# Marks of the feed-forward part: inner columns on partitions, turned in 32x32 blocks on VectorE

## The chip, the core and the metric

The kernel runs on one core of one Trainium2 chip. Its engines are TensorE (PE in the profile, its weight loads PEld), VectorE (DVE), ScalarE (ACT), GpSimd (POOL) and SyncE (SP, which here only issues transfers). They run side by side and wait for each other on semaphores. The metric is device time in microseconds; the time before is 880.39 us, the median of 3 runs (879.23 to 880.98).

## What is computed

Four sequences of 512 tokens with 512 features go through attention and then through a feed-forward layer that is sparse by a choice within blocks. The second half is what the change touches:

```python
x = layernorm(x + attention(x))                     # 4 x 512 x 512
inter = x @ c1.T @ c2.T                             # rank 16: 512 -> 16 -> 1792
idx = argmax(inter in 56 blocks of 32, axis=-1)     # one inner column for each block
h = relu(sum_m w1[idx] * x)                         # only the chosen columns
x = layernorm(x + h @ w2t[idx])
```

The kernel does not gather. It multiplies with all of w1, and sets to zero what is not the largest of its block (of equal ones it keeps the first).

## The kernel before, in words

`_attend` does the attention and `_feed_forward` the rest. The feed-forward part takes the batches b = 0 to 3 in turn, and each in 14 rounds m of 128 inner columns; a batch has 512 tokens. Every 32-bit product is made of three matmuls of high and low parts. Each engine has its own program, written out by hand in the order in which it runs; nothing is scheduled by a tool.

TensorE's round m of batch b is: `inner_up(b, m)`, 12 matmuls of 512 columns into `ps_h` (before and after it splits into two halves of six); between the halves the first of the round's preparation steps; `first_marks(b, m)`, one matmul of the marks with a triangular matrix into `ps_z`, whose entries are 1 only at the first mark of a block; `inner_down` of the round before, 12 matmuls into the four output banks `ps_pair`, with the round's second preparation step between its halves; and last `turn_mask` for the next round, four 128x128 transposes of the marks into `ps_t`.

ScalarE applies relu to `ps_h` (L933), copies the turned marks from `ps_t` to `mask_t` (L926, function `turn`), and makes the high part `g_h` of the picked values (L940). VectorE multiplies the relu's output by (ps_z == 1), which is `pick` (L1013). GpSimd makes the low part `g_l` (L883, function `low_g`); in batch 0 it also makes the low parts of w2 (L875). `inner_down` waits for `g_l`.

The preparation steps of a batch are listed in `slot_steps`. Four (s = 0 to 3) transpose the next batch's normalized tokens and split them into high and low parts; one (U) multiplies them with c1 into `u`, 80 rows; 16 (`marks(c, t)`) make the marks: for a tile of 128 tokens and a piece of 448 of the 1792 inner columns, one matmul with tokens on the partitions (L1128), a maximum over each block of 32 (L998, 14 results) and a comparison with it (L1003), which writes a 16-bit mask. All read one PSUM bank, `ps_prep`, and TensorE waits before each for VectorE's work on the one before. VectorE does a round's first step ahead of its pick.

Within a batch b of 1 to 3 VectorE has more in rounds 0 to 2: `add(b-1)` (four additions, L1028), `statistics(b-1)` (L1033, L1039, L1041), and `norm` (L1047), each for the output of the batch before.

The way in to the rounds is a stretch in which TensorE projects the attention's output of batches 1 to 3 (`project_out`, L1141) and VectorE adds the residual (`add_residual`, L1020, L1022), normalizes (`norm`, L1047) and does batch 0's first preparation steps (`front`). SyncE stores each normalized batch and loads the next residual; batch 1's tokens for step s = 0 are loaded (L799) after all four stores have landed.

Of the kernel before, what the change touches and what calls it, by code (L numbers as in the profile page):

```python
# [27 lines left out]
P = 128  # L28
# [677 lines left out]
def _feed_forward(nc, x, x1, out, w2, w2_late, sums, rden, keep, late):  # L706
# [8 lines left out]
    marks = lambda c, t: TT + 1 + c * TT + t  # L715
    att_parts2, y0, pairs = late
    att_h, att_l = zip((xt_h[1], xt_l[1]), (xt_h[0], xt_l[0]), att_parts2, (xt_h[1], xt_l[1]))
    with ExitStack() as ctx:
# [14 lines left out]
        top = [sb(f"top{j}", [P, CH // BLK]) for j in range(2)]  # L733
        mask = sb("mask", [P, TT, INTER], BF16)
# [9 lines left out]
        ps_h, ps_z, ps_prep = ps("ps_h", [P, S]), ps("ps_z", [P, S]), ps("ps_prep", [P, S])  # L744
        ps_t = ps("ps_t", [P, S], BF16)
# [3 lines left out]
        mask_turned, mask_t_ready = sem("mask_turned"), sem("mask_t_ready")  # L749
# [15 lines left out]
        def slot_steps(b, m):  # L765

            own = {0: ((1, 0), (1, 1)), 1: ((1, 2), (1, 3)), 2: ((2, 0),), 3: ((2, 1),), 4: ((2, 2),),
                   5: ((2, 3),), 6: ((3, 0), (3, 1)), 7: ((3, 2), (3, 3))}
            ahead = {2: (0,), 3: (1,), 4: (2,), 5: (3,), 8: (U,), 9: (marks(0, 0),), 10: (marks(0, 1),),
                     11: (marks(0, 2),), 12: (marks(0, 3),)}  # L770
            out = [(b, marks(c, t)) for c, t in own.get(m, ())]
            if b < NB - 1:
                out += [(b + 1, s) for s in ahead.get(m, ())]
            return out

        FRONT = [*range(TT), U, *(marks(0, t) for t in range(TT))]
# [10 lines left out]
        def front_bank(s):  # L787

            return (ps_prep, ps_z)[FRONT.index(s) % 2]

# [129 lines left out]
        def _(act):  # L920
            def turn(b, m):
                i = b * MT + m
                act.wait_ge(mask_turned, i + 1)
                if i >= 2:
                    act.wait_ge(z_done, i - 1)
                nc.scalar.activation(mask_t[m % 2][:], ps_t[:], ACT.Copy).then_inc(mask_t_ready, 1)  # L926

# [36 lines left out]
            turn(0, 0)  # L964
            high_w2(0)
            for b in range(NB):
                for m in range(MT):
                    if b == 0 and m + 1 < MT:
                        high_w2(m + 1)
                    relu(b, m)  # L970
                    if b * MT + m + 1 < NB * MT:
                        turn(*divmod(b * MT + m + 1, MT))
                    high_g(b, m)

        @block.vector
        def _(dve):
            def step(b, s, bank):
                n = number(b, s)
                dve.wait_ge(prep_mm, n + 1)
                if s < TT:  # L980
# [7 lines left out]
                    dve.wait_ge(prep_half, n + 1)  # L988
                    nc.vector.tensor_tensor(dst[1], src, dst[0].bitcast(F32), ALU.subtract).then_inc(prep_done, 1)  # L989
                elif s == U:  # L990
                    nc.vector.tensor_copy(u[:], bank[0:80]).then_inc(prep_half, 1)
                    dve.wait_ge(prep_half, n + 1)
                    nc.vector.tensor_tensor(u[32:32 + RANK], bank[32:32 + RANK],
                                            u[32:32 + RANK].bitcast(F32), ALU.subtract).then_inc(prep_done, 1)
                else:
                    c, t = divmod(s - TT - 1, TT)
                    src = bank[:, 0:CH].rearrange("p (n k) -> p n k", k=BLK)
                    nc.vector.tensor_reduce(top[t % 2][:], src, AX.X, ALU.max).then_inc(prep_half, 1)  # L998
                    dve.wait_ge(prep_half, n + 1)
                    if b and t == 0:  # L1000

                        dve.wait_ge(mask_turned, MT * (b - 1) + min(MT, -(-(c + 1) * CH // P)))
                    nc.vector.tensor_tensor(  # L1003
                        mask[:, t, c * CH:(c + 1) * CH].rearrange("p (n k) -> p n k", k=BLK), src,
                        top[t % 2][:].rearrange("p (n o) -> p n o", o=1).broadcast_to([P, CH // BLK, BLK]),
                        ALU.is_equal).then_inc(prep_done, 1)
# [43 lines left out]
            def front(s):  # L1050
                step(0, s, front_bank(s))
# [28 lines left out]
            for b in range(NB):  # L1080
                for m in range(MT):
                    steps = slot_steps(b, m)
                    if steps:
                        step(*steps[0], ps_prep)
                    pick(b, m)
                    if len(steps) > 1:
                        step(*steps[1], ps_prep)
# [18 lines left out]
        def _(pe):  # L1106
            def step(b, s, bank, banks=1):
                n = number(b, s)
                if n >= banks:
                    pe.wait_ge(prep_done, n - banks + 1)  # L1110
# [14 lines left out]
                else:  # L1125
                    c, t = divmod(s - TT - 1, TT)
                    pe.wait_ge(prep_done, number(b, U) + 1)
                    last = nc.tensor.matmul(bank[:, 0:CH], u[:, t * P:(t + 1) * P], c2_s[:, c * CH:(c + 1) * CH],  # L1128
                                            start=True, stop=True)
                last.then_inc(prep_mm, 1)  # L1130

            def front(s):
                step(0, s, front_bank(s), 2)
# [10 lines left out]

            def turn_mask(b, m):
                i = b * MT + m

                pe.wait_ge(prep_done, number(b, marks(-(-(m + 1) * P // CH) - 1, TT - 1)) + 1)
                if i:
# [145 lines left out]
```

## Time and profile before

| | |
|---|---|
| median of 3 runs | 880.39 us |
| the profiled execution, whole | 878.44 us |
| its span, from the first to the last instruction | 876.7 us |
| TensorE busy in the span | 840.4 us (96%) |
| VectorE busy | 564.4 us (64%) |
| ScalarE busy | 416.9 us (48%) |
| GpSimd busy | 279.4 us (32%) |
| a residual's load (1024 KB), median from issue to landing | 5.5 us |

The profile shows one execution. Busy time is time in which an engine had an instruction under way. Matmuls overlap, so a matmul's duration (0.39 us) is longer than the step from one start to the next (0.23 us): what a matmul costs TensorE is read from starts. An engine's idle time costs nothing unless it holds up the engine that is needed next.

### The profile page before, as it was taken

To read this page: it belongs to the slowest core of one execution; us is meant where nothing else is said; L and a number is where in the kernel's file an instruction comes from. 1 tells how busy PE (TensorE), PEld (TensorE's weight loads), DVE (VectorE), ACT (ScalarE), POOL (GpSimd) and SP (SyncE) were. 2 spreads that over 40 slices of the span, in tenths; PEclk is the share of its full clock that TensorE was granted. 3 is DMA by queue.
4 is the path that set the end of the run, shared out by engine and by line. 5 is a ranking of instruction groups with operands and counts; after the bars stand their busy time and mean duration, and the time that the engine had idled before them with its cause. 6 is when DMAs were issued, how large, how long until landed. Compare 5 with 4: busy or idle time off the path is not lost. (4 is left out here: it accounts for less than half of the span.)

```text
span 876.7 us, 11899 instructions
## 1 busy us (share of the span) xinstructions
PE 840.4 (96%) x4316; PEld 501.7 (57%) x4344; DVE 564.4 (64%) x772; ACT 416.9 (48%) x777; POOL 279.4 (32%) x324
## 2 busy tenths in 40 slices
PE   6999999999999999999989899999999999999995
PEld 5866333333333333333347677777777777777773
DVE  5588899899999999997037965328432663345304
ACT  4321677787888788878721133332222222222231
POOL 2213235633564354114304134332112211212121
PEclk9999899999999999999999899999999999999998
DMA  7793342334553453333226433110400030002001
GB/s 215 258 285 112 101 103 81 99 110 114 152 147 111 113 145 118 85 87 100 97 80 202 156 120 97 37 49 13 133 1 1 0 121 1 1 1 96 1 1 48
DMA packets 48225, 83.07 MB, mean 95 GB/s; under 512 B 9544, under 2 KB 13640, under 8 KB 48040
## 3 DMA queue, kind: packets, MB, share of 16 engines
q1 hardware_dynamic: 40448, 64.45, 23.9%
q0 software_dynamic: 7440, 16.76, 6.3%
q10 hardware_dynamic: 280, 1.11, 0.4%
q8 instruction: 35, 0.57, 0.3%
q14 instruction: 22, 0.18, 0.1%
HBM read 54.18 MB, written 28.05 MB: 94 GB/s over the span
## 5 line engine op out<-in xcount | busy, mean ns | idle before, releaser
L517 DVE TENSOR_REDUCE neg_max<-ps_pair 128x2 f32<-128x1024 f32 x256 | 303.4, 1217 | 29.9 <-PE ps_pair L632 29.7
L483 ACT ACTIVATE probs<-ps_st 128x512 f32<-128x512 f32 x512 | 267.1, 603 | 69.9 <-PE ps_st L645 69.8
L645 PE MATMUL ps_st<-q,k 50*128 50x512 f32 x512 | 158.1, 476 | 0.5 <-ACT probs L483 0.2
L883 POOL TENSOR_TENSOR g_l<-picked,g_h 128x512 fp32r<-128x512 f32 x56 | 73.1, 1306 | 268.0 <-ACT g_h L940 268.0
L645 PEld LDWEIGHTS ps_st<-q,k 50*128 50x128 f32 x512 | 69.5, 186 | 144.8 <-ACT probs L483 141.1
L659 PE MATMUL ps_pv<-probs,v 128*32 128x512 f32 x1024 | 138.3, 612 | 0.0
L926 ACT ACTIVATE mask_t<-ps_t 128x512 bf16<-128x512 bf16 x56 | 33.4, 597 | 169.0 <-PE ps_t L1152 169.0
L632 PE MATMUL ps_pair<-k,q 48*128 48x512 f32 x512 | 106.0, 448 | 7.6 <-DVE neg_max L517 7.5
L998 DVE TENSOR_REDUCE top<-ps_prep 128x14 f32<-128x448 f32 x62 | 38.6, 623 | 98.8 <-PE ps_prep L1128 98.7
L1164 PE MATMUL ps_h<-xt_h,w_h 128*128 128x512 f32 x224 | 92.4, 413 | 0.0
L1013 DVE SCALAR_TENSOR_TENSOR picked<-ps_z,picked 128x512 f32<-128x512 f32 x56 | 38.7, 691 | 77.9 <-ACT picked L933 77.8
L1164 PE MATMUL ps_h<-xt_h,w_l 128*128 128x512 f32 x224 | 87.8, 392 | 0.0
L1164 PE MATMUL ps_h<-xt_l,w_h 128*128 128x512 f32 x224 | 87.6, 391 | 0.0
L933 ACT ACTIVATE picked<-ps_h 128x512 f32<-128x512 f32 x56 | 33.6, 600 | 110.5 <-PE ps_h L1164 110.5
L632 PEld LDWEIGHTS ps_pair<-k,q 48*128 48x128 f32 x512 | 54.2, 188 | 48.4 <-DVE neg_max L517 30.8
L1189 PE MATMUL ps_pair<-w_h,g_h 128*128 128x512 f32 x160 | 71.4, 446 | 0.0
L1189 PE MATMUL ps_pair<-w_h,g_l 128*128 128x512 f32 x160 | 63.2, 395 | 0.0
L1189 PE MATMUL ps_pair<-w_l,g_h 128*128 128x512 f32 x160 | 62.5, 390 | 0.0
L311 POOL DMA_DIRECT2D maxima<-max_rows x32 | 24.7, 772 | 108.8 <-PE ps_st L645 79.1
L321 POOL DMA_DIRECT2D q<-maxima x64 | 32.4, 514 | 79.5 <-DMA maxima<-max_rows 79.3
L1164 PEld LDWEIGHTS ps_h<-xt_h,w_l 128*128 128x128 f32 x224 | 42.0, 188 | 9.3
L1164 PEld LDWEIGHTS ps_h<-xt_h,w_h 128*128 128x128 f32 x224 | 42.3, 189 | 7.1
(146 smaller groups left out, 1144.2 us busy)
## 6 DMA issues: line engine op xcount, KB each, us to landing
operands<-parts POOLq DMA_DIRECT2D x20, 512.0 KB, 4.0
q<-operands SPq DMA_DIRECT2D x64, 128.0 KB, 2.6
sums<-stage SPq DMA_DIRECT2D x32, 256.0 KB, 2.3
x_raw<-xT SPq DMA_DIRECT2D x16, 256.0 KB, 5.0
k<-operands SPq DMA_DIRECT2D x64, 64.0 KB, 2.4
q<-operands SPq DMA_DIRECT2D x64, 64.0 KB, 2.5
att<-sums SPq DMA_DIRECT2D x16, 256.0 KB
yf<-x SPq DMA_DIRECT2D x4, 1024.0 KB, 5.5
```

What stands on the lines that cost most here:

```text
L483: nc.scalar.activation(probs[kt % 2][:, r], ps_st[i % 3][:], ACT.Exp, scale=float(HD) ** -0.5).then_inc(exp_done, 1)
L517: nc.vector.tensor_reduce(neg_max[:, at:at + 2], ps_max[pair % 2][:], AX.X, ALU.max, negate=True).then_inc(max_red, 1)
L632: nc.tensor.matmul(ps_max[tile // 2 % 2][:, a], q[n % QR][64 * a:64 * a + STACK, j, t * P:(t + 1) * P], k_[n % QR][64 * a:64 * a + STACK, ...
L645: nc.tensor.matmul(ps_st[i % 3][:], k_[n % QR][64 * a:64 * a + ROWS, kt * P:(kt + 1) * P], q[n % QR][64 * a:64 * a + ROWS, j, :], start=Tr ...
L659: last = nc.tensor.matmul(ps_pv[32 * r:32 * r + VW], v[b][:, kt, g], probs[kt % 2][:, r], start=(kt == 0), stop=(kt == TT - 1))
L883: nc.gpsimd.tensor_tensor(g_l[m % 2][:], picked[m % 2][:], g_h[m % 2][:].bitcast(F32), ALU.subtract).then_inc(g_ready, 1)
L926: nc.scalar.activation(mask_t[m % 2][:], ps_t[:], ACT.Copy).then_inc(mask_t_ready, 1)
L933: nc.scalar.activation(picked[m % 2][:], ps_h[:], ACT.Relu).then_inc(relu_ready, 1)
L998: nc.vector.tensor_reduce(top[t % 2][:], src, AX.X, ALU.max).then_inc(prep_half, 1)
L1013: nc.vector.scalar_tensor_tensor(picked[m % 2][:], ps_z[:], 1.0, picked[m % 2][:], ALU.is_equal, ALU.mult).then_inc(picked_ready, 1)
L1164: last = nc.tensor.matmul(ps_h[:], w[:, k, m * P:(m + 1) * P], xx[b % 2][:, k], start=(k == 0 and n == 0), stop=(k == KT - 1 and n == 2))
L1189: last = nc.tensor.matmul(ps_out[t][:], g[m % 2][:, t * P:(t + 1) * P], w2_tile(*w, m), start=(m == 0 and n == 0), stop=(m == MT - 1 and n ...
```

## The change

The marks are computed with inner columns on the partitions and tokens along the free dimension. A marks step now belongs to a round: `marks(m)` is one matmul of the 128 inner columns of round m with all 512 tokens (weights `c2_s`, moving data `u`), so 14 of 512 columns take the place of 16 of 448. VectorE then turns the bank in 32x32 blocks from PSUM into `turned`, which brings the 32 columns of an inner block to lie along the free dimension; it takes the maximum of each group of 32 (16 results), compares, which writes `marked` in 16 bits, and turns the blocks back into `mask_t`. TensorE's `turn_mask` (four transposes a round) and ScalarE's `turn` (one copy a round) are gone, and with them `ps_t` and the 14 KB `mask`.

Further: `u` has two buffers, by batch; the preparation steps use two banks in turn and TensorE waits for the step before the last; each round r does the marks of round r+1; VectorE does its pick first, then the marks, then the second step. On the way in one marks step stands in place of four, and VectorE's first `add_residual` of batch 2 stands ahead of batch 1's `norm`.

```diff
         def slot_steps(b, m):
...
-            own = {0: ((1, 0), (1, 1)), 1: ((1, 2), (1, 3)), 2: ((2, 0),), 3: ((2, 1),), 4: ((2, 2),),
-                   5: ((2, 3),), 6: ((3, 0), (3, 1)), 7: ((3, 2), (3, 3))}
...
+            ahead = {2: 0, 3: 1, 4: 2, 5: 3, 8: U}
+            following = (b, marks(m + 1)) if m + 1 < MT else (b + 1, marks(0))
...
+        def prep_bank(b, s):
+
+            return ps_prep[number(b, s) % 2]
...
-            def turn(b, m):
-                i = b * MT + m
-                act.wait_ge(mask_turned, i + 1)
-                if i >= 2:
-                    act.wait_ge(z_done, i - 1)
-                nc.scalar.activation(mask_t[m % 2][:], ps_t[:], ACT.Copy).then_inc(mask_t_ready, 1)
...
-                    nc.vector.tensor_reduce(top[t % 2][:], src, AX.X, ALU.max).then_inc(prep_half, 1)
...
+                    i = b * MT + s - TT - 1
+                    if i:
+                        dve.wait_ge(marks_ready, i)
+                    nc.vector.transpose(turned[:].rearrange("p n k -> p (n k)"), bank[:]).then_inc(prep_done, 1)
+                    dve.wait_ge(prep_done, n + 1)
+                    nc.vector.tensor_reduce(top[:], turned[:], AX.X, ALU.max).then_inc(topped, 1)
+                    dve.wait_ge(topped, i + 1)
+                    if i:
+                        dve.wait_ge(mask_t_ready, i)
                     nc.vector.tensor_tensor(
...
+                        marked[:], turned[:],
+                        top[:].rearrange("p (n o) -> p n o", o=1).broadcast_to([P, S // BLK, BLK]),
+                        ALU.is_equal).then_inc(marks_ready, 1)
+                    dve.wait_ge(marks_ready, i + 1)
+                    if i >= 2:
+                        dve.wait_ge(z_done, i - 1)
+                    nc.vector.transpose(mask_t[i % 2][:], marked[:].rearrange("p n k -> p (n k)")).then_inc(mask_t_ready, 1)
...
-            front(marks(0, 0))
-            front(marks(0, 1))
+            front(marks(0))
+            add_residual(2, 0)
             norm(1)
-            add_residual(2, 0)
-            front(marks(0, 2))
-            front(marks(0, 3))
...
                     steps = slot_steps(b, m)
+                    pick(b, m)
                     if steps:
-                        step(*steps[0], ps_prep)
-                    pick(b, m)
+                        step(*steps[0])
...
-                    last = nc.tensor.matmul(bank[:, 0:CH], u[:, t * P:(t + 1) * P], c2_s[:, c * CH:(c + 1) * CH],
-                                            start=True, stop=True)
+                    last = nc.tensor.matmul(bank[:], c2_s[:, m * P:(m + 1) * P], us[b % 2][:], start=True, stop=True)
...
-                    if b * MT + m + 1 < NB * MT:
-                        turn_mask(*divmod(b * MT + m + 1, MT))
```

On VectorE, from batch 1's pick of round 1 to its pick of round 2, before (marks steps L998 and L1003, statistics L1033 to L1041):

```order
L1013 SCALAR_TENSOR_TENSOR picked<-ps_z,picked 128x512 [waits relu_ready,z_done]
L998 TENSOR_REDUCE top<-ps_prep 128x14 [waits prep_mm]
L1003 TENSOR_TENSOR mask<-ps_prep,top 128x448 [waits prep_half]
L1033 BN_STATS statsf<-yf 128x6 [waits yf_ready] x4
L1039 BN_AGGR mvf<-statsf 128x2 [waits statf_done] x4
L1041 TENSOR_SCALAR varf<-mvf 128x4 [waits aggrf_done]
L998 TENSOR_REDUCE top<-ps_prep 128x14 [waits prep_mm]
L1003 TENSOR_TENSOR mask<-ps_prep,top 128x448 [waits mask_turned,prep_half]
L1013 SCALAR_TENSOR_TENSOR picked<-ps_z,picked 128x512 [waits relu_ready,z_done]
```

The same engine after the change, from one pick to the next in a round of batch 0 with a token step (marks L991 to L1004, token step L978 and L980):

```order
L1011 SCALAR_TENSOR_TENSOR picked<-ps_z,picked 128x512 [waits relu_ready,z_done]
L991 STREAM_TRANSPOSE turned<-ps_prep 128x512 [waits marks_ready,prep_mm]
L993 TENSOR_REDUCE top<-turned 128x16 [waits prep_done]
L997 TENSOR_TENSOR marked<-turned,top 128x512 [waits mask_t_ready,topped]
L1004 STREAM_TRANSPOSE mask_t<-marked 128x512 [waits z_done,marks_ready]
L978 CAST xt_h<-ps_prep 128x4x128 [waits prep_mm]
L980 TENSOR_TENSOR xt_l<-ps_prep,xt_h 128x4x128 [waits prep_half]
L1011 SCALAR_TENSOR_TENSOR picked<-ps_z,picked 128x512 [waits relu_ready,z_done]
```

A marks step has grown from two instructions to four, each waiting for the one before it, and stands behind the pick.

On TensorE, the end of one round and the start of the next, before:

```order
L1189 MATMUL ps_pair<-w_h,g_l 128x512
L1152 MATMUL ps_t<-ident,mask 128x128 [waits mask_t_ready,prep_done]
L1152 MATMUL ps_t<-ident,mask 128x128 x3
L1164 MATMUL ps_h<-xt_h,w_h 128x512 [waits relu_ready]
L1164 MATMUL ps_h<-xt_l,w_h 128x512
```

and after:

```order
L1173 MATMUL ps_pair<-w_h,g_l 128x512
L1148 MATMUL ps_h<-xt_h,w_h 128x512 [waits relu_ready]
L1148 MATMUL ps_h<-xt_l,w_h 128x512
L1148 MATMUL ps_h<-xt_h,w_l 128x512
L1148 MATMUL ps_h<-xt_h,w_h 128x512
```

The four transposes between the rounds are gone; the rest of the round keeps its order.

## Rows read from the trace of the kernel before

**Rows 1.** Busy time in a stretch of rounds: length, engines, clock, DMA, GB/s

```profile
620.00:700.00 80.00, 80.00 (x381) 61.45 (x387) 35.19 (x60) 20.92 (x37) 16.32 (x14) 1.00 0.08 25
```

**Rows 2.** Waits, 515 to 877 us, TensorE's: us in total, times, longest

```profile
PE ps_pair L1189 <- POOL g_l L883: 0.5, 1, 0.5
```

**Rows 3.** Timeline of TensorE at a round's end: start us, us, what

```profile
844.55 0.39 PE L1189 MATMUL ps_pair<-w_h,g_l 128*128 128x512 f32 x1
844.78 0.40 PE L1152 MATMUL ps_t<-ident,mask 128*128 128x128 bf16 x4
844.99 0.48 PE L1164 MATMUL ps_h<-xt_h,w_h 128*128 128x512 f32 x1
845.31 0.39 PE L1164 MATMUL ps_h<-xt_l,w_h 128*128 128x512 f32 x1
```

**Rows 4.** Timeline of TensorE at a marks matmul

```profile
691.42 0.37 PE L1128 MATMUL ps_prep<-c_s,u 80*128 80x448 f32 x1
691.63 0.40 PE L1164 MATMUL ps_h<-xt_h,w_h 128*128 128x512 f32 x1
```

**Rows 5.** TensorE's groups by form, 515 to 877 us: busy us, mean ns

```profile
L1152 PE MATMUL ps_t<-ident,mask 128*128 128x128 bf16 x212 | 21.1, 222 | 0.0
L1128 PE MATMUL ps_prep<-c_s,u 80*128 80x448 f32 x55 | 20.2, 368 | 0.0
```

**Rows 6.** VectorE's groups by form, whole span

```profile
L1013 DVE SCALAR_TENSOR_TENSOR picked<-ps_z,picked 128x512 f32<-128x512 f32 x56 | 38.7, 691 | 77.9 <-ACT picked L933 77.8
L539 DVE STREAM_TRANSPOSE max_rows<-max_parts 128x32 f32<-128x32 f32 x32 | 6.4, 201 | 0.1
```

**Rows 7.** Timelines of VectorE and GpSimd in the attention, 259 to 264 us

```profile
260.95 0.91 DVE L532 TENSOR_TENSOR max_parts<-neg_max,max_parts 128x16 fp32r<-128x16 f32 x1
262.92 0.19 DVE L539 STREAM_TRANSPOSE max_rows<-max_parts 128x32 f32<-128x32 f32 x1
...
260.56 1.27 POOL L384 TENSOR_TENSOR att<-att,inv 128x512 f32<-128x512 f32 x1
...
262.59 1.28 POOL L390 TENSOR_TENSOR xt_l<-att,xt_h 128x512 fp32r<-128x512 f32 x1
```

**Rows 8.** Timeline of the last round: relu, pick, low part

```profile
860.10 0.60 ACT L933 ACTIVATE picked<-ps_h 128x512 f32<-128x512 f32 x1 [1.69 <-PE ps_h L1164]
860.80 0.69 DVE L1013 SCALAR_TENSOR_TENSOR picked<-ps_z,picked 128x512 f32<-128x512 f32 x1 [5.35 <-ACT picked L933]
862.24 1.28 POOL L883 TENSOR_TENSOR g_l<-picked,g_h 128x512 fp32r<-128x512 f32 x1 [2.46 <-ACT g_h L940]
```

**Rows 9.** Timeline of VectorE in a batch's first rounds

```profile
603.74 2.46 DVE L1033 BATCH_NORM_STATS2 statsf<-yf 128x6 f32<-128x512 f32 x4
...
606.60 0.61 DVE L998 TENSOR_REDUCE top<-ps_prep 128x14 f32<-128x448 f32 x1
607.25 0.62 DVE L1003 TENSOR_TENSOR mask<-ps_prep,top 128x448 bf16<-128x448 f32 x1
...
610.58 1.91 DVE L1047 TENSOR_SCALAR yf<-yf,mvf,rstdf 128x512 f32<-128x512 f32 x4
...
690.01 2.48 DVE L1028 TENSOR_TENSOR yf<-ps_pair,yf 128x512 f32<-128x512 f32 x4 [0.18 <-PE ps_pair L1189]
```

**Rows 10.** Timelines of the way in: VectorE, SyncE's issues, TensorE

```profile
479.69 3.90 DVE L1047 TENSOR_SCALAR yf<-yf,mvf,rstdf 128x512 f32<-128x512 f32 x4
...
495.68 0.68 DVE L1020 TENSOR_TENSOR yf<-ps_pair,yf 128x512 f32<-128x512 f32 x1
...
504.48 3.85 DVE L1047 TENSOR_SCALAR yf<-yf,mvf,rstdf 128x512 f32<-128x512 f32 x4
...
487.80 0.38 SPq L820 DMA_DIRECT2D yf<-x  x1
...
513.08 0.33 SPq L799 DMA_DIRECT2D xf_sb<-after_attention  x1
...
516.12 0.60 PE L1118 MATMUL ps_prep<-ident,xf_sb 128*128 128x128 f32 x4
```

More of the change, by code:

```diff
@@ L732, in _feed_forward @@
         x_sb = [sb(f"xf_sb{j}", [P, D]) for j in range(2)]
[L733 to L734 removed]
+        u_next = sb("u_next", [80, S], F32R)
+        turned = sb("turned", [P, S // BLK, BLK])
+        top = sb("top", [P, S // BLK])
+        marked = sb("marked", [P, S // BLK, BLK], BF16)
         mask_t = [sb(f"mask_t{j}", [P, S], BF16) for j in range(2)]
@@ L765, in slot_steps @@
         def slot_steps(b, m):
-            own = {0: ((1, 0), (1, 1)), 1: ((1, 2), (1, 3)), 2: ((2, 0),), 3: ((2, 1),), 4: ((2, 2),),
-                   5: ((2, 3),), 6: ((3, 0), (3, 1)), 7: ((3, 2), (3, 3))}
[L769 to L773, printed above, removed]
+            ahead = {2: 0, 3: 1, 4: 2, 5: 3, 8: U}
+            following = (b, marks(m + 1)) if m + 1 < MT else (b + 1, marks(0))
+            out = [following] if following[0] < NB else []
+            if b + 1 < NB and m in ahead:
+                out.append((b + 1, ahead[m]))
             return out
-        FRONT = [*range(TT), U, *(marks(0, t) for t in range(TT))]
+        FRONT = [*range(TT), U, marks(0)]
         ORDER = [(0, s) for s in FRONT]
@@ L1050, in front @@
             def front(s):
-                step(0, s, front_bank(s))
+                step(0, s)
             add_residual(0, 0)
@@ L1106, in _, with step @@
         def _(pe):
[L1107 to L1110, printed above, removed]
+            def step(b, s):
+                n, bank = number(b, s), prep_bank(b, s)
+                if n >= 2:
+                    pe.wait_ge(prep_done, n - 1)
                 if s < TT:
@@ L1143, in project_out @@
                 last.then_inc(wo_done, 1)
[L1145 to L1149, printed above, removed]
-                    pe.wait_ge(mask_t_ready, i)
-                for t in range(TT):
-                    last = nc.tensor.transpose(ps_t[:, t * P:(t + 1) * P], mask[:, t, m * P:(m + 1) * P], ident16[:])
-                last.then_inc(mask_turned, 1)
             def inner_up(b, m, ks):
@@ L1205, in _ @@
             project_out(2, 2)
-            front(marks(0, 0))
-            front(marks(0, 1))
+            front(marks(0))
             project_out(2, 3)
-            front(marks(0, 2))
-            front(marks(0, 3))
-            project_out(3, 0)
-            project_out(3, 1)
-            turn_mask(0, 0)
-            project_out(3, 2)
-            project_out(3, 3)
+            for t in range(TT):
+                project_out(3, t)
             inner_up(0, 0, (0, 1, 2, 3))
@@ L1223, in _ @@
                     if steps:
-                        step(*steps[0], ps_prep)
+                        step(*steps[0])
                     if b * MT + m:
```

45 lines of the change are left out of this document (17 added, 28 removed).

## The prediction

> **What bounds the kernel now.** I read the busy time by stretches first. In the rounds TensorE is busy all of the time (80.00 of 80.00 us between 620 and 700) at a granted clock of 1.00, and VectorE less than half (35.19) [rows 1]. The list of waits for 515 to 877 us then has one wait of a matmul, 0.5 us in the last round [rows 2]; the other engines wait for TensorE. So in some 360 us the sum of what TensorE issues is the time, and what is taken off its queue is gained whole, as long as the others keep up. The question of this change is whether VectorE does. The way in, 480 to 515 us, is different: there VectorE is the late one, and it ends in a transfer [rows 10].
>
> **What goes on TensorE.** A round's end shows the cost of `turn_mask`. From the last matmul of `inner_down` at 844.55 to the transposes at 844.78 is an ordinary step, 0.23. The transposes hold the queue to 844.99, and the matmul behind them takes 0.32 to the next instead of 0.23 (845.31) [rows 3]. So four transposes cost 845.31 - 844.78 - 0.23 = 0.30 us. I count from one fixed point, the first token step of batch 1 (516.12, in round 2 of batch 0 [rows 10]), since from there on the order is regular. Behind it stand 53 groups of four (212 transposes [rows 5]): 53 x 0.30 = **-15.9**. A marks matmul of 448 columns takes 691.63 - 691.42 = 0.21 [rows 4], and there are 55 [rows 5]: 11.5. In their place come 52 of 512 columns at the ordinary 0.23, 12.0: **+0.5**. The token steps, U, `first_marks` and all others stay as they are.
>
> **What it costs VectorE.** Nothing in the trace is a 32x32 turn of 512 columns. Its nearest row is the turn of 32 columns, 201 ns [rows 6]. Two readings bound it. If the instruction pays a fixed part and then one element after another, as the others do (the pick takes 691 ns for 512 [rows 6], the maximum 610 for 448 [rows 9]: about 0.16 us and 1.04 ns an element), 32 elements should take 0.19, and they do; 512 would take 0.70. If each block of 32 paid the whole 201 ns, 16 blocks would take 3.2 us. Below, two elements at a time, like the norm (1.91 for four of 512, 0.48 each [rows 9]), would be 0.5. I take 0.70 since it explains the row. Maximum and comparison of 512 elements are 0.70 each by the same line. Between two that depend on each other lie 0.04 us (606.60 + 0.61 to 607.25 [rows 9]).
>
> The Trainium skill ("VectorE: DVE Perf Modes", section "The three transpose paths") gives 311 ns for VectorE's turn of 128x128 in bf16. An estimate that takes four of them for 512 columns is 1.24 us; one that takes 0.16 us as fixed is 0.76. With 1.24 twice a round the sum below would come out some 7 us longer.
>
> **A collision that the change makes.** The comparison used to read PSUM; now it reads two tiles in SBUF. The trace shows what happens to such an instruction beside GpSimd: L532, which takes 0.17 us alone, started at 260.95 while GpSimd's L384 ran from 260.56 to 261.83, and lasted 0.91, to 261.86, so it was held to GpSimd's end. The 32x32 turn at 262.92 took its usual 0.19 in the middle of GpSimd's L390 [rows 7]. So the turns go free, and the comparison doesn't. The four norms of the way in show the same, 3.90 and 3.85 us beside GpSimd [rows 10] against 1.91 [rows 9]. Now place it: with the pick at P, the low part `g_l` runs from P+1.44 (860.80 to 862.24) to P+2.72 [rows 8]. Until now ScalarE's `turn` lay between, and `g_l` came later. The marks chain is: turn P+0.69 to 1.39, maximum 1.43 to 2.13, comparison ready at 2.17, held to 2.72, done 0.56 later at P+3.28, turn back to **P+4.0**. Without the hold it would be P+3.6. No row shows a maximum over SBUF data beside GpSimd. The skill ("SBUF — State Buffer", "Who interferes with whom") says a reduction never contends on this chip; here it starts ahead of `g_l` anyway.
>
> **Does it fit in a round?** A plain round is now 24 x 0.2285 + 0.23 + 0.23 = 5.95 us, one with a token step 6.4. With a round's start at T, the matmuls of `inner_up` end at T+2.97, and relu and pick follow: P = T+3.9 (the last round: 0.9 from that end to 860.80 [rows 8]). `first_marks` of the next round wants the marks at T+5.95+2.97 = T+8.9, and they are there at T+7.9. So the slack is 1.0 us, and a token step behind them (two of 0.69, to T+9.3) still ends ahead of the next pick. `g_l` is ready at T+6.6 and wanted at T+9.1. Ten rounds of each batch, and all of batch 0, cost nothing.
>
> The first rounds of batches 1 to 3 don't fit so well. There VectorE adds 2.4, then 606.60 - 603.74 = 2.86 of statistics, then 1.91 of norm, and in rounds 2 and 3 a token step of 1.4 [rows 9]. Laid out from the batch's start at 0: pick 3.9, marks 7.9, additions 10.3; pick 10.3 (0.5 late), marks 14.3, statistics 17.2; pick 17.2 (1.4 late), marks 21.2, just when TensorE wants them (18.3 + 2.97); token step 22.6, norm 24.5; pick 24.4 (2.3 late), marks 28.4, wanted at 24.7 + 2.97 = 27.6: TensorE stands 0.8 us. A round later VectorE has caught up. Batch 3 has no token steps, so rounds are shorter, and the wait is 0.4 in round 3. Together **+2.1**. Here what hides the chain is gone: each 0.1 us more on a turn costs about 1.2 us in all.
>
> **The way in.** Batch 2's residual is ready late because of batch 1's norm (479.69, 3.90 long, beside GpSimd) and four marks steps around it. Now one chain of about 3 to 4 us (its comparison meets GpSimd too) stands for four steps of 1.2, and the norm runs partly past GpSimd's work. By VectorE alone batch 3's additions (495.68) would start 2.4 us earlier. But their data are loaded after batch 1's norm is stored; that norm ends about 1.2 later than now, since one chain and an addition stand ahead, so the load issued at 487.80 comes at 489.0 and lands some 5.5 later (the median of the table) at 494.5: 1.2 earlier, not 2.4. From there to batch 3's norm VectorE has pick and one chain (4.0) in place of two steps and a pick (3.0), and the norm meets one GpSimd instruction, not two (2.4 against 3.85): 0.5 less. Its store is followed by the load at 513.08 and the token step at 516.12, 3 us behind [rows 10]; TensorE gets there earlier than the data. So **-1.7**. Bounds: 0, if the loads move no further, and -4, if no hold occurs.
>
> **Sum.** -15.9 + 0.5 + 2.1 - 1.7 = -15.0. The profiled execution took 878.44 and would take 863.4; it lies 1.95 under the median, and I set the same difference against that: 880.4 - 15.0 = **865.4 us**. The end of the kernel is unchanged.
>
> **Rivals.**
> *All hidden.* The comparison isn't held, or the chain is some tenths shorter (a 16-bit turn at two elements at a time): no stand in rounds 3, and 1.5 more on the way in. 880.4 - 15.9 + 0.5 - 3.2 = 861.8. For it: the slack lacks only 0.8. Against: [rows 7].
> *The gap stays.* Of the 0.30 only the 0.21 of the transposes go, and the 0.09 behind them belongs to the round's start with its wait for relu: 53 x 0.09 = 4.8 back, 870.2. Against: the step behind a token step's transposes is just as long and has no such wait.
> *Turns dearer.* 0.9 to 1.3 us each: +2.5 to +8.4, 868 to 874. Only the 32-column row stands against it.
> *VectorE becomes the bound (slower).* With 3.2 us a turn a round of VectorE is 0.69 + 6.4 + 1.4 + gaps, about 8.7 us against TensorE's 5.95, and the rounds run at VectorE's pace: batch 0 takes 40 us more than planned and the others 48 each, so some 180 us more, 1045 us. It decides from about 1.5 us a turn: there the first four rounds of each batch lose what the transposes gave. Against: 201 ns for 32 elements would then hold no fixed part.
> *The change doesn't relieve TensorE.* If its clock fell for want of work in the new waits, matmuls would be slower; but by the layout above it never stands over 1 us, and the granted clock is 1.00 in [rows 1]. I give this no chance of its own.
>
> **How the numbers follow.** Forecast as summed, 863.5 to 867.5: 0.45. All hidden, to 861.5: 0.18. Gap stays, 870: 0.11. Turns dearer, 868 to 874: 0.15. VectorE the bound: 0.07. Something else on the way in, near 880: 0.04. Leaving out 2 in 10 at the dear end, the range is 861.0 to 872.5. A measurement of this kernel can tell about 0.2% (1.8 us) from no change. Faster by more: 0.91; within: 0.02; slower: 0.07.
>
> **What would show it.** In the profile after: turns of 0.70 us on VectorE; the comparison near 1.1 us in plain rounds beside `g_l`; a pick-to-pick of TensorE's plain rounds of 5.95; matmul waits for `mask_t` only in rounds 3 of batches 1 to 3, under 1 us each; the first token step of batch 1 near 514.4. The prediction is wrong if waits for the marks stand in plain rounds, if the turns take over 0.9, or if TensorE's round is over 6.0 without a wait.

## The result and the profile after

The changed kernel takes **865.92 us** (median of 4 runs, 863.11 to 868.45) beside 879.81 us of the kernel before (4 runs, 877.24 to 880.98). The ratio is 0.9834, 95% interval 0.9805 to 0.9862: 1.7% faster, and 0.5 us above the forecast of 865.4.

The page of the changed kernel begins (span, then busy time, share of the span, instructions of each engine):

```profile
span 866.7 us, 11538 instructions
PE 826.0 (95%) x4112; PEld 493.9 (57%) x4112; DVE 664.3 (77%) x868; ACT 390.3 (45%) x721; POOL 284.6 (33%) x324
```

VectorE has 100 us more than before and ScalarE 27 us less. TensorE has 14.4 us less, and is still the engine that the others wait for. Two stretches of rounds (length, then busy us of PE, PEld, DVE, ACT, POOL, then TensorE's granted clock, the DMA share and GB/s), which answer to [rows 1]:

```profile
620.00:700.00 80.00, 79.42 (x353) 62.38 (x352) 59.03 (x84) 15.41 (x25) 17.98 (x14) 1.00 0.08 24
700.00:780.00 80.00, 79.20 (x351) 61.90 (x350) 59.03 (x81) 15.37 (x25) 15.64 (x12) 1.00 0.09 30
```

VectorE went from 35 of 80 us to 59, and TensorE is no longer busy all of the time: some 0.6 us are missing in the first stretch and 0.8 in the second. The clock stays at 1.00. The list of waits, 512 to 866 us, says what they are (total us, times, longest), and answers to [rows 2]:

```profile
PE ps_prep L1118 <- DVE turned L991: 1.7, 3, 0.6
PE ps_pair L1173 <- POOL g_l L884: 0.5, 1, 0.5
PE ps_z L1159 <- DVE mask_t L1004: 0.4, 2, 0.2
```

The second is the old one. The third is the wait for the marks that I forecast, though smaller: TensorE lost 0.38, 0.37 and 0.17 us at that place in batches 1 to 3. The first, step U waiting for VectorE's turn of the marks, I hadn't foreseen. A round's end on TensorE, which answers to [rows 3], has an even step of 0.23 from one round to the next:

```profile
560.88 0.39 PE L1173 MATMUL ps_pair<-w_h,g_l 128*128 128x512 f32 x1
561.11 0.39 PE L1148 MATMUL ps_h<-xt_h,w_h 128*128 128x512 f32 x1
561.34 0.39 PE L1148 MATMUL ps_h<-xt_l,w_h 128*128 128x512 f32 x1
```

VectorE's groups by form, 515 to 866 us (busy us, mean ns of one, idle time before), show the new marks step:

```profile
L997 DVE TENSOR_TENSOR marked<-turned,top 128x512 bf16<-128x512 f32 x53 | 64.6, 1218 | 1.8
L1004 DVE STREAM_TRANSPOSE mask_t<-marked 128x512 bf16<-128x512 bf16 x54 | 38.4, 712 | 1.8
L991 DVE STREAM_TRANSPOSE turned<-ps_prep 128x512 f32<-128x512 f32 x53 | 37.4, 705 | 0.0
L993 DVE TENSOR_REDUCE top<-turned 128x16 f32<-128x512 f32 x53 | 36.4, 686 | 1.8
```

**Where the time went.** Single executions differ in the attention, whose code is the same: the first `add_residual` of the way in began at 450.37 us in the profile before and at 454.94 in the one after. So I compare two stretches that don't contain it. The way in is from that addition to batch 1's first token step, and the rounds are from that step to the end of the span. Before, that step is the last row of [rows 10]; after, it is the second row here:

```profile
454.94 0.69 DVE L1018 TENSOR_TENSOR yf<-ps_pair,yf 128x512 f32<-128x512 f32 x1 [38.00 <-PEq L91]
518.59 0.63 PE L1113 MATMUL ps_prep<-ident,xf_sb 128*128 128x128 f32 x4
```

| | before | after | moved | forecast |
|---|---|---|---|---|
| attention, to the first addition | 450.37 | 454.94 | +4.6 | 0 |
| way in | 65.75 | 63.65 | -2.1 | -1.7 |
| rounds, to the end | 360.6 | 348.1 | -12.5 | -13.3 |
| span | 876.7 | 866.7 | -10.0 | -15.0 |

The profiled execution after was the slowest of its four (868.45), and its attention is where it was slow; the medians differ by 13.9 us.

### The profile page after: what moved, and what is told of

Its sections match the earlier page's. It is cut to its first block and busy times, and to the rows that moved or that the text cites. A ratio compares the mean times of both kernels' runs of the same rounds, so it can differ in the third digit from the quotient of the medians.

```text
span 866.7 us, 11538 instructions
## 1 busy us (share of the span) xinstructions
PE 826.0 (95%) x4112; PEld 493.9 (57%) x4112; DVE 664.3 (77%) x868; ACT 390.3 (45%) x721; POOL 284.6 (33%) x324
## 5 line engine op out<-in xcount | busy, mean ns | idle before, releaser
L1148 PE MATMUL ps_h<-xt_h,w_h 128*128 128x512 f32 x224 | 87.8, 392 | 0.2 <-ACT picked L927 0.2
L632 PEld LDWEIGHTS ps_pair<-k,q 48*128 48x128 f32 x512 | 54.2, 189 | 50.2 <-DVE neg_max L517 33.4
L997 DVE TENSOR_TENSOR marked<-turned,top 128x512 bf16<-128x512 f32 x56 | 68.4, 1222 | 1.9
L934 ACT ACTIVATE g_h<-picked 128x512 fp32r<-128x512 f32 x56 | 35.4, 632 | 62.7 <-DVE picked L1011 62.7
L1148 PEld LDWEIGHTS ps_h<-xt_l,w_h 128*128 128x128 f32 x224 | 42.2, 189 | 9.2
```

The lines of the kernel that those rows point to most:

```text
L632: nc.tensor.matmul(ps_max[tile // 2 % 2][:, a], q[n % QR][64 * a:64 * a + STACK, j, t * P:(t + 1) * P], k_[n % QR][64 * a:64 * a + STACK, ...
L934: nc.scalar.activation(g_h[m % 2][:], picked[m % 2][:], ACT.Copy).then_inc(g_high, 1)
L997: nc.vector.tensor_tensor(marked[:], turned[:], top[:].rearrange("p (n o) -> p n o", o=1).broadcast_to([P, S // BLK, BLK]), ALU.is_equal). ...
L1148: last = nc.tensor.matmul(ps_h[:], w[:, k, m * P:(m + 1) * P], xx[b % 2][:, k], start=(k == 0 and n == 0), stop=(k == KT - 1 and n == 2))
```

## The experiments

My theory after the first look: the rounds take longer than what TensorE issues there (their floor), because VectorE is late in two places, step U (0.8 us in each of batches 0 to 2) and `first_marks` behind the norm (0.4 in each of batches 1 to 3). The comparison's hold by GpSimd has a share in the second. The rivals: the excess lies in something that no wait shows (longer matmuls, for one); or the comparison is slow of itself, reading two tiles in SBUF, and GpSimd has no part in it.

All kernels below are judged by the stretch of the rounds first, which two profiles of the changed kernel give as 348.1 and 348.1, while its runs scatter by 6 us.

### U waits for the token steps alone

In the profile after, step U stands here on TensorE and on VectorE:

```profile
555.96 0.40 PE L1173 MATMUL ps_pair<-w_h,g_l 128*128 128x512 f32 x1
556.94 0.43 PE L1118 MATMUL ps_prep<-xt_h,c_h 128*80 128x512 f32 x1 [0.58 <-DVE turned L991]
...
555.48 0.69 DVE L1011 SCALAR_TENSOR_TENSOR picked<-ps_z,picked 128x512 f32<-128x512 f32 x1 [1.94 <-ACT picked L927]
556.09 0.71 DVE L991 STREAM_TRANSPOSE turned<-ps_prep 128x512 f32<-128x512 f32 x1
```

An ordinary step would have started U at 556.19, 0.23 behind 555.96. It started at 556.94, right behind the end of the turn (556.09 + 0.71), so it lost 0.75, and as much in batches 1 and 2. U needs the token steps' results and its own bank, but the code waits for every preparation step ahead of it, and since the change one of them is the marks step of the same round, which VectorE begins only after its pick.

```diff
                 elif s == U:
-                    pe.wait_ge(prep_done, n)
+                    pe.wait_ge(prep_done, number(b, TT - 1) + 1)
```

> The changed kernel with one wait altered: TensorE's step U (the product with c1) waits for the four token steps that it reads and no longer for every preparation step ahead of it, of which the last is the marks step whose turn stands behind the pick. Theory: the wait of 0.6 us in the profile, some 0.8 us with the start of the matmul behind it, goes in each of batches 0 to 2: from the first token step of batch 1 to the end 345.8 in place of 348.1 us, whole kernel 2.4 us shorter. Rival: U was not the last thing that TensorE waits for there, and the next wait (for the marks in first_marks) takes its place: no change.

The rounds took 858.5 - 512.72 = 345.8 us, 2.3 less than in the changed kernel, and U's waits are gone from the list; the waits for `mask_t` stay (0.5 us in two). Median 863.16, ratio 0.9806 (0.9756 to 0.9855).

### The low part by memset

GpSimd writes zeros to `g_l` instead of subtracting: the low part of the picked values is left out.

```diff
-                nc.gpsimd.tensor_tensor(g_l[m % 2][:], picked[m % 2][:], g_h[m % 2][:].bitcast(F32),
-                                        ALU.subtract).then_inc(g_ready, 1)
+                nc.gpsimd.memset(g_l[m % 2][:].bitcast(F32), 0.0).then_inc(g_ready, 1)
```

> The changed kernel with GpSimd's low part g_l left out: a memset of zeros in its place (512 columns, reads nothing), so g_l adds nothing to the output. Theory of the hold: the comparison on VectorE (1.22 us in all 56 rounds) waits for GpSimd's reads from SBUF, so it drops to 0.69 us where no w2 part runs beside it, and the waits of TensorE for mask_t (2.5 us) go; from the first token step of batch 1 to the end about 346.0 us. Rival: a comparison of two SBUF tiles with a broadcast is slow by itself; then it stays at 1.22 and so do the waits.

Its groups of VectorE by form, 610 to 863 us (batches 1 to 3, where GpSimd has nothing else beside the comparison):

```profile
L996 DVE TENSOR_TENSOR marked<-turned,top 128x512 bf16<-128x512 f32 x38 | 26.3, 692 | 1.3
```

All 38 comparisons take 0.69. There is no wait for `mask_t`, and U's three waits stay at 1.7 in all. The rounds took 346.4: 1.7 less than the changed kernel. Of that some 1.1 are the waits for the marks, and the rest is the last round's wait for `g_l` (0.5 before and after), which a short memset takes away. Median 863.56, ratio 0.9812 (0.976 to 0.9863).

### The low part behind the comparison

The same work in full, but GpSimd starts `g_l` only when the next marks are made.

```diff
+                if i + 1 < NB * MT:
+                    pool.wait_ge(marks_ready, i + 2)
                 nc.gpsimd.tensor_tensor(g_l[m % 2][:], picked[m % 2][:], g_h[m % 2][:].bitcast(F32),
```

> The changed kernel, but GpSimd starts a round's low part g_l only when the comparison of the next marks is done. Hold theory: the comparison takes 0.69 us in batches 1 to 3, the marks chain is 0.5 us shorter, while g_l is ready 1.4 us later; in plain rounds it is in time (wanted 9.1 us after the round's start, ready at 8.1), in rounds 2 to 4 of batches 1 to 3 TensorE now waits for g_l in place of the marks, 1 to 2 us a batch. Stretch from the first token step of batch 1 to the end 347 to 351 us. Rival (slow by itself): comparison stays at 1.22, stretch over 351.

A plain round of it, on VectorE and GpSimd:

```profile
533.51 0.69 DVE L999 TENSOR_TENSOR marked<-turned,top 128x512 bf16<-128x512 f32 x1
534.24 0.71 DVE L1006 STREAM_TRANSPOSE mask_t<-marked 128x512 bf16<-128x512 bf16 x1
...
534.34 1.30 POOL L886 TENSOR_TENSOR g_l<-picked,g_h 128x512 fp32r<-128x512 f32 x1 [3.86 <-issue]
```

The subtraction now lies beside the turn back, and neither is longer for it. The comparison takes 0.69, all 52 of them. So it is the meeting of these two instructions that costs 0.53 us, and the turn is free of it. The rounds took 347.2, 0.9 less, which is what TensorE lost at `first_marks` in the changed kernel; the waits for `mask_t` are gone, and the waits for `g_l` that I had thought possible in the crowded rounds did not come. Median 864.3, ratio 0.9819 (0.9768 to 0.9869).

### Marks ahead of the pick

```diff
-                    pick(b, m)
                     if steps:
                         step(*steps[0])
+                    pick(b, m)
```

> The changed kernel with VectorE's order in a round as before: marks first, then the pick. Theory: the chain starts when the marks matmul is done, 2 us after the round's start, so it ends at 4.8 and the pick moves from 3.9 to 4.8; the comparison then lies ahead of the round's g_l and behind the last one's, is not held (0.69 us), U finds the turn done, and the backlog of rounds 0 to 3 stays under what TensorE can bear. Waits for mask_t and at U gone: stretch 343.5 to 345 us, kernel 3 to 4.5 us shorter than the changed one. Rival: the pick is what counts, and its delay of 0.9 us makes TensorE wait for g_l in rounds 1 to 4: stretch 348 us or more.

The list of waits of TensorE, 518 to 862 us, has one line left:

```profile
PE ps_pair L1173 <- POOL g_l L884: 0.5, 1, 0.5
```

The rounds took 861.8 - 517.08 = **344.7** us. This is the floor: nothing in TensorE's queue waits for VectorE there. The comparison takes 0.693, since GpSimd's subtraction comes behind the pick and so behind the marks. In this kernel the marks don't need the relu's output, and VectorE makes them while it would wait for ScalarE. Median 864.88, ratio 0.9826 (0.9775 to 0.9876).

### One more turn in each marks step

```diff
+                    nc.vector.transpose(turned[:].rearrange("p n k -> p (n k)"), bank[:]).then_inc(turned_once, 1)
+                    dve.wait_ge(turned_once, i + 1)
                     nc.vector.transpose(turned[:].rearrange("p n k -> p (n k)"), bank[:]).then_inc(prep_done, 1)
```

> The changed kernel with the turn out of PSUM done twice in each marks step, into the same tile: 0.75 us more in the chain. Theory (VectorE's backlog in rounds 0 to 3 of batches 1 to 3 is what it costs): by the layout with a turn of 1.05 us in place of 0.70 some 1.1 to 1.6 us more in each of these batches, and the wait at U 0.7 longer in batches 0 to 2; from the first token step of batch 1 to the end 348.1 + 6 = 354 us (352.5 to 356). Rival: the chain has room in every round, and only U's wait grows: 350.2 us. Rival: the chain is on the path in every round: over 385 us.

One round of it on VectorE, and TensorE's list of waits, 520 to 873 us:

```profile
526.52 0.71 DVE L992 STREAM_TRANSPOSE turned<-ps_prep 128x512 f32<-128x512 f32 x1
527.26 0.72 DVE L994 STREAM_TRANSPOSE turned<-ps_prep 128x512 f32<-128x512 f32 x1
```

```profile
PE ps_prep L1121 <- DVE turned L994: 4.0, 3, 1.3
PE ps_z L1162 <- DVE mask_t L1007: 2.1, 6, 0.7
```

The rounds took 874.0 - 520.19 = 353.8, 5.7 more than the changed kernel. A chain that is 0.74 longer costs more than 0.74 in each of U's and `first_marks`' crowded places (9 waits, 6.1 us in all, for 2.1 in the changed kernel), and nothing in the plain rounds. The median rose to 872.51, 5 to 7 us over the changed kernel's two medians; ratio 0.9899 (0.9852 to 0.9946). So with one of the two turns at 1.4 us the change would still have been a gain, of 1.0% instead of 1.7%. A chain 0.74 longer is two turns of 1.07; at the prediction's 1.2 us for each 0.1 that makes 4.4, and 5.7 were measured. The prediction had no price for U, whose three waits grew by 2.3.

### Statistics and norm in rounds 6 and 7

```diff
-                    if b and m == 1:
+                    if b and m == 6:
                         statistics(b - 1)
-                    if b and m == 2:
+                    if b and m == 7:
                         norm(NB + b - 1)
...
-                    if b and m == 3:
+                    if b and m == 8:
                         store(NB + b - 1, flat(out, b - 1), y[0], out_sent)
-                    if b and m == 5:
+                    if b and m == 10:
                         load_y(b)
```

GpSimd's inverse root, which stands between the two, moves with them.

> The changed kernel with the statistics and the norm of the batch before moved from rounds 1 and 2 to rounds 6 and 7 of batches 1 to 3 (its store and the next load to rounds 8 and 10). Theory of the backlog: TensorE's six late starts on mask_t go, 2 to 2.5 us; stretch from the first token step of batch 1 to the end 345.5 to 346.3 us (348.1 before), with U's waits left. Rival: the waits are due to the additions of round 0 alone; then they stay.

**This one missed.** The rounds took 866.6 - 518.28 = 348.3 us instead of 345.5 to 346.3. The waits for `mask_t` are gone, as expected, but U's have grown:

```profile
PE ps_prep L1118 <- DVE turned L991: 2.9, 3, 1.2
```

The reason lies in this part of its timeline of VectorE and TensorE:

```profile
642.86 1.87 DVE L1045 TENSOR_SCALAR yf<-yf,mvf,rstdf 128x512 f32<-128x512 f32 x4
644.65 0.68 DVE L1011 SCALAR_TENSOR_TENSOR picked<-ps_z,picked 128x512 f32<-128x512 f32 x1
645.25 0.70 DVE L991 STREAM_TRANSPOSE turned<-ps_prep 128x512 f32<-128x512 f32 x1
...
646.10 0.43 PE L1118 MATMUL ps_prep<-xt_h,c_h 128*80 128x512 f32 x1 [1.17 <-DVE turned L991]
```

The norm now stands in round 7, just ahead of U's round 8, and makes the turn that U waits for 0.6 us later, in batches 1 and 2 alike. The lateness was moved from one consumer to another. (The median of these four runs, 862.39, ratio 0.9798 (0.9744 to 0.9852), looks like a gain; the stretch of the rounds says that the move brought none.)

### Norm ahead of the first addition on the way in

```diff
-            add_residual(2, 0)
             norm(1)
+            add_residual(2, 0)
```

> The changed kernel with one edit undone on the way in: batch 1's norm ahead of the first addition of batch 2, as before. Theory (what ends last there is the chain of norm, store, load): the norm ends 1.3 us earlier, and so the residual of batch 3 is there 1.3 us earlier; TensorE idles 3 us longer ahead of batch 3's projection but is not the last. From VectorE's first addition behind the attention to the first token step of batch 1: 62.4 to 63.4 us (63.65 with the change, 65.75 before). Rival (TensorE's projection is the late one there): 65.5 us or more. The rest of the run is unchanged, 348.1 us.

The rival held: the way in took 516.08 - 449.93 = 66.15 us, 2.5 more than in the changed kernel. TensorE's list for the way in of the changed kernel, and of this one:

```profile
PE ps_pair L1135 <- DVE yf L1018: 7.1, 3, 3.9
```

```profile
PE ps_pair L1135 <- DVE yf L1018: 8.7, 2, 4.8
```

With the norm (3.06 us here) first, the addition that frees a bank for `project_out` comes 3 us later, and TensorE stands 4.8 us there in one piece instead of 2.0 and 1.2. What I had counted as a small price, one addition ahead of the norm, is what keeps TensorE's projection going. The rest of the chain (pick, norm, store, load, step) then follows a later TensorE: the pick waits 1.5 us for a relu, and batch 3's norm begins 56.4 us after the first addition, for 54.2 in the changed kernel. Median 866.52, ratio 0.9832 (0.9789 to 0.9875).

### The kernel before, with only the new place of the pick

```diff
                     steps = slot_steps(b, m)
+                    pick(b, m)
                     if steps:
                         step(*steps[0], ps_prep)
-                    pick(b, m)
```

> The kernel before with one part of the change alone: VectorE's pick ahead of the round's first preparation step. Theory: with one bank for all steps TensorE's second step waits for VectorE's work on the first, which now ends near 5.9 us after the round's start where TensorE wants it at 4.6: 1.3 to 1.4 us in each of some 27 rounds with two steps, stretch from the first token step of batch 1 to the end 360.6 + 33 = 394 us. Rival: VectorE has room (35 of 80 us busy), so the order doesn't matter: 360.6 us.

The rounds took 913.8 - 520.35 = 393.5 us instead of 360.6 (one run, 915.54 us). TensorE's waits, 520 to 912 us:

```profile
PE ps_prep L1128 <- DVE mask L1003: 14.8, 14, 1.1
PE ps_prep L1118 <- DVE mask L1003: 12.6, 12, 1.1
```

In 26 rounds the second step of a round waits, each for 1.05 us, because with one bank it can't start before VectorE has done the first, and the first now stands behind the pick. These waits make 27.4 us. So the order by itself is a loss of 33 us, by one execution. In the changed kernel, where TensorE waits for the step before the last, such waits are absent; that its second bank is what spares them follows from the code, but no run took that bank away.

### Both at once, and the changed kernel once more

The two edits for U and for the norm together, five rounds, beside the unaltered changed kernel on the same chip.

> The changed kernel with both: U waits for the token steps alone, and a batch's statistics and norm stand in rounds 6 and 7 (its store in 8, the next residual's load in 10). Theory (the 3.4 us by which the rounds of the changed kernel are over those of the kernel with the marks first, 348.1 against 344.7, are U's waits, 2.3, and the waits for mask_t behind the norm, 1.1; with the norm in round 7 U waited longer, 2.9 against 1.7, because U stands in round 8): both go, the stretch from batch 1's first token step to the end is 344.7 to 345.0, TensorE has no wait for VectorE behind that step, and the time is 862 to 863, 3.3 below the changed kernel on the same chip. Rival (something else than these waits is longer in the changed kernel, for example the matmuls themselves): 346 or more in that stretch with no waits in the list.

> The changed kernel once more, unaltered, beside the one above on one chip. Every theory: the stretch from batch 1's first token step to the end is 348.0 to 348.3 again, with U's three waits of 0.6. The way in (first addition to that step) lies between 62.9 and 64.7, as in the three kernels so far that have the same code there, against 65.75 in the kernel before; if it came out at 65.5 or more, the 2.1 us gained there would be chance. The first addition starts anywhere from 448 to 455.5, as it did before.

| | rounds | way in | median us (runs) | ratio to before |
|---|---|---|---|---|
| both edits | 861.9 - 517.21 = 344.7 | 64.1 | 863.63 (861.22 to 865.26) | 0.9809 (0.9781 to 0.9836) |
| changed kernel again | 866.0 - 517.85 = 348.1 | 63.6 | 867.32 (862.97 to 869.82) | 0.9848 (0.9817 to 0.988) |

With both, the rounds are at the floor, and TensorE's list is again the one line of the kernel with the marks first. The norm's move, which gave nothing alone, gives 1.1 us once U doesn't wait for it. The changed kernel repeats its 348.1. By the rounds this kernel and the one with the marks first are the best of those run, 3.4 us under the changed one. The medians of the two kernels in the table differ by 3.7, but their ratios' intervals overlap, so that gain is shown by the rounds and not by the medians.

## Why the forecast was right, and where not

**What goes on TensorE.** The floor of the rounds is 344.7, with no wait for VectorE. That is 15.9 less than before, where I had -15.9 + 0.5 = -15.4. With the marks' +0.5 as forecast, a group of transposes was worth 16.4 / 53 = 0.31 us instead of 0.30. The rival that the gap behind them stays is refuted by the even steps at 560.88, 561.11 and 561.34.

**The price of a turn.** 0.705 us from PSUM in 32 bits, and 0.712 from SBUF in 16 bits; forecast 0.70. The straight line through other instructions' sizes held, from the one row of 32 columns in [rows 6]. The size of the elements made no difference, so a part of the rival "all hidden" (two 16-bit elements at a time) fell. Maximum and unheld comparison took 0.686 and 0.692 for 0.70.

The Trainium skill ("VectorE: DVE Perf Modes", section "The three transpose paths") gives 311 ns for 128x128 in bf16. An estimate of four times that is 1.24 us for 512 columns; the trace has 0.71. The estimate that counts a fixed part of 0.16 us once, 0.76, is near it.

**The collision.** The comparison was held in all 56 marks steps (1.19 to 1.47 us, the middle one 1.22), as [rows 7] had suggested from a much smaller instruction. In the profile after, one round on VectorE and GpSimd:

```profile
602.47 0.69 DVE L993 TENSOR_REDUCE top<-turned 128x16 f32<-128x512 f32 x1
603.19 1.21 DVE L997 TENSOR_TENSOR marked<-turned,top 128x512 bf16<-128x512 f32 x1
...
602.56 1.30 POOL L884 TENSOR_TENSOR g_l<-picked,g_h 128x512 fp32r<-128x512 f32 x1 [5.00 <-ACT g_h L934]
```

GpSimd ends at 603.86, and the comparison 0.54 later, where I had 0.56. The two experiments with the low part show that it is this overlap. The Trainium skill ("SBUF — State Buffer", "Who interferes with whom") has the rule: a VectorE instruction with two inputs in SBUF contends with a GpSimd one that reads SBUF, and a reduction doesn't. The trace agrees for both: the comparison is held to 1.22 from 0.69, and the maximum, which also reads SBUF, lies beside `g_l` from 602.56 on and still takes 0.69, as all 56 do, while `g_l` takes its usual 1.30.

**Does it fit.** Plain rounds: 5.96 us for the forecast 5.95, with no waits. Here is the crowded place of batch 1 on VectorE, then TensorE's marks and `first_marks` steps:

```profile
607.90 0.69 DVE L1011 SCALAR_TENSOR_TENSOR picked<-ps_z,picked 128x512 f32<-128x512 f32 x1
...
612.54 0.69 DVE L980 TENSOR_TENSOR xt_l<-ps_prep,xt_h 128x512 fp32r<-128x512 f32 x1
613.15 1.91 DVE L1045 TENSOR_SCALAR yf<-yf,mvf,rstdf 128x512 f32<-128x512 f32 x4
614.97 0.69 DVE L1011 SCALAR_TENSOR_TENSOR picked<-ps_z,picked 128x512 f32<-128x512 f32 x1
...
618.29 0.71 DVE L1004 STREAM_TRANSPOSE mask_t<-marked 128x512 bf16<-128x512 bf16 x1
...
617.06 0.40 PE L1123 MATMUL ps_prep<-u_next,c_s 80*128 80x512 f32 x1
619.06 0.39 PE L1159 MATMUL ps_z<-mask_t,first 128*128 128x512 bf16 x1 [0.22 <-DVE mask_t L1004]
623.87 0.40 PE L1123 MATMUL ps_prep<-u_next,c_s 80*128 80x512 f32 x1
```

The backlog is where I put it: norm, pick, marks, and TensorE waits in round 3. With the pick of round 1 (601.14 in the trace) taken as the layout's 10.3, the layout puts the next two at 608.0 and 615.2; they started at 607.90 and 614.97. The chain from pick to marks is 619.00 - 614.97 = 4.03, forecast 4.0. TensorE's step from one marks matmul to the next is 623.87 - 617.06 = 6.81 there, and 6.41 in the round before (610.65 to 617.06): 0.40 lost. Batch 2 lost nearly as much, and batch 3, forecast at 0.4, lost 0.17. **The step that was mis-sized** is this one: 0.8 forecast for a batch with token steps, 0.4 measured. The reason is a difference of two numbers near 28: the layout put the marks at 28.4 and they came 0.25 earlier, while TensorE, which it put at 27.6, would have taken them at 27.8 (619.06 - 0.40 in the trace). VectorE is earlier since its instructions that don't depend on each other start up to 0.1 us before the one ahead has ended (612.54 + 0.69 = 613.23, and the next begins at 613.15). In all three batches the wait took 1.1 (the norm's move once U no longer waits, 345.8 to 344.7), not 2.1 (the prediction's own parts, 0.8, 0.8 and 0.4, make 2.0).

**The step that was left out** is U: 2.3 us in three batches. The prediction says "The token steps, U, `first_marks` and all others stay as they are." U's wait line did stay as it was; what it waits for did not. Before, no marks step stood in U's round (round 8 had U alone); since the change each round has one, and it comes behind the pick. I had asked, of the moved work, who waits for `mask_t`, and not who waits for `prep_done`, which the same chain sets at its first instruction. Missed 2.3 and overrated 1.0: the stand of TensorE was 3.4 us for 2.1.

**The way in.** 2.1 us gained for 1.7 forecast, by one profile of before. Four more kernels with the same code there gave 64.7, 62.85, 64.1 and 63.6, so a single one of these is good to about 1 us, and the gain lies somewhere between 1.0 and 2.9. How I came to it is only in part borne out. The load of batch 3's residual is the late one before its additions, as I had it. These rows are VectorE's, SyncE's and TensorE's:

```profile
487.16 2.94 DVE L1045 TENSOR_SCALAR yf<-yf,mvf,rstdf 128x512 f32<-128x512 f32 x4
499.47 0.69 DVE L1018 TENSOR_TENSOR yf<-ps_pair,yf 128x512 f32<-128x512 f32 x1 [0.94 <-DMA yf<-x]
...
494.45 0.38 SPq L821 DMA_DIRECT2D yf<-x  x1
...
509.31 0.39 PE L1159 MATMUL ps_z<-mask_t,first 128*128 128x512 bf16 x1 [3.41 <-DVE mask_t L1004]
```

Counted from the first addition, the additions of batch 3 began 44.5 us on (45.3 before), and the load 39.5 (37.4 before). So the load, which the additions wait for now, was issued 2.1 later; I had put it 1.2 later. The additions came 0.8 earlier for 1.2. The rest, 1.3 us for the forecast 0.5, came between the additions and the token step. The last row is a wait of 3.4 us at `first_marks`, part of this stretch, which the prediction didn't have: it let TensorE get to the token step before the data. That was no longer so. Here are the load and the step in the changed kernel run again, where the wait was 3.5:

```profile
513.92 0.33 SPq L800 DMA_DIRECT2D xf_sb<-after_attention  x1
...
517.62 0.39 PE L1173 MATMUL ps_pair<-w_h,g_l 128*128 128x512 f32 x1
517.85 0.60 PE L1113 MATMUL ps_prep<-ident,xf_sb 128*128 128x128 f32 x4
```

The load landed 2.7 us after its issue, at 516.6, and the step began at 517.85, an ordinary 0.23 behind the matmul ahead of it. So there TensorE was the later by 1.2 us. In the first profile the two came together (data at 518.5, TensorE at 518.48), and in five others of the kernels run the step waited 0.3 to 1.2 us for its data (1.9 in the one with the norm first). The two chains end almost together, and where TensorE is the later the wait at `first_marks` isn't free. What it costs stays open; no run took it away.

**The sum.** Transposes 0.5 better, waits in the rounds 1.3 dearer (3.4 for 2.1), way in 0.4 better, which is less than its scatter. These cancel to 0.4, so the total is a better hit than its parts. That the median came within 0.5 us is luck besides: the attention's end alone moves by 7 us between executions, and the medians moved by 13.9, not by 15.0.

## What to carry to other kernels

Work moved on an engine's queue must be followed through every semaphore that it increments, at each instruction of its chain, and for each of them the waiting lines on the other engines be read again: the cost came where the code of the waiting step had not been touched. A wait that counts "all steps so far" takes in a new neighbour silently. And a crowded place should be removed only together with what waits next behind it: the norm's move was worth nothing with U's wait in place and 1.1 us without it.

## What the runs showed of the hardware

A turn of 32x32 blocks over 512 columns costs VectorE 0.71 us, from PSUM or from SBUF, little more than its pick, maximum or unheld comparison of that size (0.69). GpSimd's work beside it doesn't lengthen it: the turn out of SBUF took 0.71 us in all 56 steps of the kernel with the low part behind the comparison, where GpSimd's subtraction ran beside it.

The attention, whose instructions are the same in all these kernels, ended at very different times. The first addition behind it began between 448.0 and 455.4 us, on the whole later where the granted clock of two early stretches was lower. These are the rows for 60 to 126 and 126 to 200 us of the kernel with U's wait changed (addition at 448.02), and of the one with the norm moved (455.43):

```profile
60.00:126.00 66.00, 64.52 (x333) 32.73 (x332) 57.70 (x69) 33.65 (x64) 19.66 (x30) 0.97 0.44 119
126.00:200.00 74.00, 71.67 (x427) 24.91 (x428) 68.79 (x75) 58.35 (x113) 37.41 (x48) 1.00 0.34 97
```

```profile
60.00:126.00 66.00, 64.81 (x314) 33.38 (x312) 55.09 (x66) 30.38 (x57) 20.30 (x31) 0.90 0.38 117
126.00:200.00 74.00, 71.88 (x412) 25.54 (x408) 65.77 (x71) 56.53 (x110) 34.44 (x43) 0.95 0.32 93
```

The granted clock is 0.97 and 1.00 in the early one, 0.90 and 0.95 in the late one, and TensorE is busy for nearly the same time in both. Two more lie between: the kernel before with 0.95 and 0.98 (450.37), the changed one with 0.92 and 0.95 (454.94). The order isn't strict: the kernel with the norm first on the way in had 1.00 and 0.98, and its addition began at 449.93. What sets the clock there, the runs don't show. It is a spread as large as half of this change's gain, and it lies in code that the change doesn't touch; the stretch of the rounds, at a granted clock of 1.00, repeats to 0.1 us.
